# A BitNet attention and feed-forward layer on eight cores: deferred transposes, a third weight buffer, and PSUM copies moved to ScalarE

## The reference

```python
xn = _layernorm(x)
x = x + attention(xn, Wq, Wk, Wv, Wo) + ffn(xn, gate_w, up_w, down_w, gate_s, up_s, down_s)

def bitlinear(x, W):      # ternary weights, 8-bit activations per row
    sw = mean(abs(W)) + 1e-05
    Wq = clip(round(W / sw), -1, 1) * sw
    sx = 127 / clip(max(abs(x), axis=-1, keepdims=True), 1e-05, None)
    xq = clip(round(x * sx), -128, 127) / sx
    return einsum('bsd,od->bso', xq, Wq)
# attention: q = rope(bitlinear(x, Wq)), k = rope(bitlinear(x, Wk)), v = bitlinear(x, Wv);
#            16 query heads, 4 key/value heads of 128; causal softmax; bitlinear(out, Wo)
# ffn:       g = (x @ gate_w.T) * gate_s;  u = (x @ up_w.T) * up_s      (inner width 5632)
#            out = ((silu(g) * u) @ down_w.T) * down_s
```

## Time and profile before

| | us |
|---|---|
| median of 2 runs | 5812.83 |
| the 2 runs | 5696.64, 5929.02 |
| profiled execution, whole | 5710.21 |
| its slowest core (core 1), span | 5708.6 |
| its other cores, spans | 5672.5 to 5704.6 |

### The profile page before, as it was taken

The page is one execution under the profiler, slowest core; times in us unless marked ns, Lnnn a source line. Parts: engine busy times, 40 slices in busy tenths (PEclk is TensorE's granted clock), DMA queues, the critical chain, the costliest instruction groups (busy, mean ns, idle before and its releaser), DMA issues.

```text
span 5708.6 us, 54936 instructions; the slowest of 8 cores (5672.5 to 5708.6 us)
## 1 busy us (share of the span) xinstructions
PE 3868.1 (68%) x18728; PEld 1777.5 (31%) x18728; DVE 1691.8 (30%) x2717; ACT 1640.2 (29%) x1375; POOL 303.1 (5%) x276
## 2 busy tenths in 40 slices
PE   1899988889999886044443034445788889973068
PEld 1344434434444343032332023333222222222034
DVE  4100000000000001455555456555422211137433
ACT  4111110001111000443332421220455656653231
POOL 0111110011111000000000000000000000000000
PEclk9899999999999998567676567778999999985589
DMA  3578867768786775411112611111000000000656
GB/s 120 56 70 79 76 65 83 83 69 78 74 78 66 85 83 87 130 50 52 50 65 62 175 57 34 44 45 49 15 10 8 7 6 5 6 3 1 184 191 215
DMA packets 800203, 387.61 MB, mean 68 GB/s; under 512 B 552256, under 2 KB 777920, under 8 KB 787648
## 3 DMA queue, kind: packets, MB, share of 16 engines
q0 software_dynamic: 548608, 161.50, 26.7%
q1 hardware_dynamic: 251328, 222.61, 13.1%
HBM read 480.53 MB, written 41.94 MB: 92 GB/s over the span
## 4 chain that ended last, share of the span: by engine, by line
PE 55%; DVE 19%; DMA 10%; ACT 9%; issue 5%; DVEq 1%; ACTq 0%; SPq 0%; POOLq 0%; POOL 0%
PE f_pd_h L341 11%; PE f_pg_h L300 11%; PE f_pu_h L306 11%; PE c_pse L736 3%; PE c_ppv L740 3%; ACT c_pp L794 2%; PE e_po L943 2%; PE c_psc L785 2%; DMA wq_wb<-wq_t 2%; PE c_psc L783 2%; DMA wo_wb<-wo_t 2%; PE c_pse L738 2%; PE c_ppv L742 2%; PE b_pkv L554 2%; DVE b_mx L165 2%
## 5 line engine op out<-in xcount | busy, mean ns | idle before, releaser
L794 ACT ACTIVATE c_pp<-c_psc 128x1024 bf16<-128x1024 f32 x640 | 656.0, 1025 | 582.9 <-PE c_psc L785 582.9
L341 PE MATMUL f_pd_h<-hdnT,f_dw_h 128*128 128x512 bf16 x2816 | 639.1, 390 | 45.9 <-DMA f_dw_h<-dw_t 45.9
L300 PE MATMUL f_pg_h<-xnT,f_gw_h 128*128 128x512 bf16 x2816 | 639.4, 386 | 31.1 <-DMA f_uw_h<-uw_t 31.1
L306 PE MATMUL f_pu_h<-xnT,f_uw_h 128*128 128x512 bf16 x2816 | 635.3, 385 | 0.0
L803 DVE TENSOR_TENSOR c_pp<-c_pp,cmask 128x512 bf16<-128x512 bf16 x512 | 217.7, 425 | 799.9 <-ACT c_pp L794 770.9
L651 PE MATMUL b_pq<-b_xqT,qtern 128*128 128x256 bf16 x2048 | 270.5, 292 | 266.9 <-DVE b_qrot L660 258.3
L321 DVE TENSOR_TENSOR hdnT<-f_sg_h,f_su_h 128x1024 bf16<-128x1024 bf16 x88 | 61.0, 693 | 1219.0 <-ACT f_su_h L317 1219.0
L341 PEld LDWEIGHTS f_pd_h<-hdnT,f_dw_h 128*128 128x128 bf16 x2816 | 283.5, 101 | 391.9 <-issue 81.0
L300 PEld LDWEIGHTS f_pg_h<-xnT,f_gw_h 128*128 128x128 bf16 x2816 | 279.4, 99 | 376.6 <-issue 79.4
L306 PEld LDWEIGHTS f_pu_h<-xnT,f_uw_h 128*128 128x128 bf16 x2816 | 278.5, 99 | 342.4 <-issue 43.4
L532 PE MATMUL b_pkv<-b_xqT,ktern 128*128 128x256 bf16 x1024 | 177.4, 355 | 289.4 <-DVE b_krot L541 272.6
(11 more groups left out here) (163 smaller groups left out, 4013.2 us busy)
## 6 DMA issues: line engine op xcount, KB each, us to landing
f_gw_h<-gw_t POOLq DMA_DIRECT2D x88, 512.0 KB, 6.8
f_uw_h<-uw_t POOLq DMA_DIRECT2D x88, 512.0 KB, 8.8
f_dw_h<-dw_t POOLq DMA_DIRECT2D x32, 1408.0 KB, 16.6
b_xch<-x_kv SPq DMA_DIRECT2D x16, 2048.0 KB, 7.8
wq_wb<-wq_t SPq DMA_DIRECT2D x32, 1024.0 KB, 6.8
wo_wb<-wo_t SPq DMA_DIRECT2D x32, 1024.0 KB, 6.8
f_xch<-x_q SPq DMA_DIRECT2D x4, 4096.0 KB, 16.5
ffn_scr<-f_ffs_h SPq DMA_DIRECT2D x32, 512.0 KB, 10.6
```

The source lines that it names most:

```text
L300: e.matmul(pg[:, bi, tc * 512:(tc + 1) * 512], gwb[bi][:, dt, :], xnT[:, dt, half * HT + tc * 512: half * HT + (tc + 1) * 512], start=(dt ...
L306: e.matmul(pu[:, bi, tc * 512:(tc + 1) * 512], uwb[bi][:, dt, :], xnT[:, dt, half * HT + tc * 512: half * HT + (tc + 1) * 512], start=(dt ...
L341: e.matmul(pd[:, bi, tc * 512:(tc + 1) * 512], dwb[bi][:, it, :], hdnT[:, it, tc * 512:(tc + 1) * 512], start=(it == 0), stop=(it == NIT - 1))
L794: E("scalar", lambda e, k0=k0, sbk=sbk: e.activation(pp[:, (k0 % 8):(k0 % 8) + 2, :].rearrange("p a b -> p (a b)"), psc[sbk][:], AF.Exp, s ...
```

## The change

- F2 has three buffers each for the gate and up weights, F3 three for the down weights (`i % 3`, `h % 3`), with three semaphores each. The PSUM halves and the store buffers keep two.
- In F3 the transposes, the copies to `ffstage` and the store of step `h` become a function `f3tail` that is issued after block `h+1` (and before ACT's copy of step `h+1`); the last step's tail is issued at the end of the half. The transpose groups wait for the last copy out of their own bank (`ptf_ve[g]`), not for the newest DVE count.
- `emit_tr16` can copy out with ACT (`evac_eng="scalar"`). B1 and B2 use it so; F1 and D stay on DVE. In B1 the copy of V to `vT` is on ACT too. The lists that say when a PSUM bank is free now hold (semaphore, count) pairs.

The core of the diff:

```diff
-    def emit_tr16(src, dst_fn, ptr, src_ready_w, tag_rot, ptr_ve=None, extra_w=()):
+    def emit_tr16(src, dst_fn, ptr, src_ready_w, tag_rot, ptr_ve=None, extra_w=(),
+                  evac_eng="vector"):
...
-            E("vector", lambda e, g=g, bank=bank: e.tensor_copy(
-                dst_fn(g), bank.rearrange("p (a b) -> p a b", b=128)),
-              waits=[(pe, pe.n)], inc=(ve, 1))
...
+            else:
+                E("scalar", lambda e, g=g, bank=bank: e.activation(
+                    dst_fn(g), bank.rearrange("p (a b) -> p a b", b=128), AF.Identity),
+                  waits=[(pe, pe.n), (ac, ac.n)], inc=(ac, 1))
+                if ptr_ve is not None:
+                    ptr_ve[bi] = (ac, ac.n)
...
-                    gwb = [sb(f"f_gw{i}_h{half}", [128, NDT, 128], BF16, f2) for i in range(2)]
-                    uwb = [sb(f"f_uw{i}_h{half}", [128, NDT, 128], BF16, f2) for i in range(2)]
+                    gwb = [sb(f"f_gw{i}_h{half}", [128, NDT, 128], BF16, f2) for i in range(3)]
+                    uwb = [sb(f"f_uw{i}_h{half}", [128, NDT, 128], BF16, f2) for i in range(3)]
...
-                          waits=[(pe, wpe[bi])] + (fence if i < 2 else []), inc=(s_gw[bi], 16))
+                          waits=[(pe, wpe[wb])] + (fence if i < 3 else []), inc=(s_gw[wb], 16))
...
-                          waits=[(pe, dpe[bi])] + (fence3 if h < 2 else []), inc=(s_dw[bi], 16))
+                          waits=[(pe, dpe[wb])] + (fence3 if h < 3 else []), inc=(s_dw[wb], 16))
...
+                        dpe[wb] = pe.n
+                        if f3pend[0] is not None:
+                            f3pend[0]()
+                            f3pend[0] = None
+                        E("scalar", lambda e, h=h, pb=pb: e.activation(fft[:], pd[:, pb, :], AF.Identity,
                                                                        scale=c_ds[:, h:h + 1]),
                           waits=[(pe, pe.n)], inc=(ac, 1))
...
+                        def f3tail(h=h, pb=pb, half=half, FOK=FOK):
+                            for g in range(2):
+                                E("tensor", lambda e, g=g: [
+                                    e.transpose(ptf[:, g % 2, j * 128:(j + 1) * 128],
+                                                fft[:, (g * 4 + j) * 128:(g * 4 + j + 1) * 128],
+                                                c_identf[:]) for j in range(4)][-1],
+                                  waits=[FOK, (ve, ptf_ve[g]), (s_fst[pb], stv[pb])], inc=(pe, 1))
+                                E("vector", lambda e, g=g, pb=pb: e.tensor_copy(
+                                    ffstage[pb][:, g * 4:(g + 1) * 4, :].rearrange("p a b -> p (a b)"),
+                                    ptf[:, g % 2, :]),
+                                  waits=[(pe, pe.n)], inc=(ve, 1))
+                                ptf_ve[g] = ve.n
+                            E("sync", lambda e, h=h, pb=pb, half=half: e.dma_start(
...
+                        f3pend[0] = f3tail
...
-                                  ptr, rdy, t, ptr_ve)
+                                  ptr, rdy, t, ptr_ve, evac_eng="scalar")
...
-                    XQT = (ve, ve.n)
+                    XQT = (ac, ac.n)
...
-                        E("vector", lambda e, t=t, c=c, pb=pb: e.tensor_copy(
-                            vT[:, c * 2 + t, :], pkv[pb][:]),
-                          waits=[(pe, pe.n), (ve, ve.n)], inc=(ve, 1))
-                        pkv_ve[pb] = ve.n
+                        E("scalar", lambda e, t=t, c=c, pb=pb: e.activation(
+                            vT[:, c * 2 + t, :], pkv[pb][:], AF.Identity),
+                          waits=[(pe, pe.n), (ac, ac.n)], inc=(ac, 1))
+                        pkv_ve[pb] = (ac, ac.n)
```

More of the change, by code:

```diff
@@ L195, in emit_tr16 @@
             bank = ptr[:, bi, :]
-            war = (ve, ptr_ve[bi]) if ptr_ve is not None else (ve, ve.n)
+            war = ptr_ve[bi] if ptr_ve is not None else (ve, ve.n)
             E("tensor", lambda e, g=g, bank=bank, src=src: [
@@ L289, in do_half @@
                         bi = i % 2
-                        E("gpsimd", lambda e, i=i, bi=bi: e.dma_start(
-                            out=gwb[bi][:], in_=gw_t[:, i * 128:(i + 1) * 128]
+                        wb = i % 3
+                        E("gpsimd", lambda e, i=i, wb=wb: e.dma_start(
+                            out=gwb[wb][:], in_=gw_t[:, i * 128:(i + 1) * 128]
                             .rearrange("(t p) f -> p t f", p=128)),
-                          waits=[(pe, wpe[bi])] + (fence if i < 2 else []), inc=(s_gw[bi], 16))
-                        E("gpsimd", lambda e, i=i, bi=bi: e.dma_start(
-                            out=uwb[bi][:], in_=uw_t[:, i * 128:(i + 1) * 128]
+                          waits=[(pe, wpe[wb])] + (fence if i < 3 else []), inc=(s_gw[wb], 16))
+                        E("gpsimd", lambda e, i=i, wb=wb: e.dma_start(
+                            out=uwb[wb][:], in_=uw_t[:, i * 128:(i + 1) * 128]
                             .rearrange("(t p) f -> p t f", p=128)),
[L297 to L300, removed]
+                          waits=[(pe, wpe[wb])] + (fence if i < 3 else []), inc=(s_uw[wb], 16))
+                        wready = [(s_gw[wb], s_gw[wb].n), (s_uw[wb], s_uw[wb].n)]
+                        E("tensor", lambda e, bi=bi, wb=wb, half=half: [
+                            e.matmul(pg[:, bi, tc * 512:(tc + 1) * 512], gwb[wb][:, dt, :],
                                      xnT[:, dt, half * HT + tc * 512: half * HT + (tc + 1) * 512],
@@ L304, in do_half @@
                           waits=wready + [(ac, silu_ac[bi])] + (fence if i < 2 else []), inc=(pe, 1))
-                        E("tensor", lambda e, bi=bi, half=half: [
-                            e.matmul(pu[:, bi, tc * 512:(tc + 1) * 512], uwb[bi][:, dt, :],
+                        E("tensor", lambda e, bi=bi, wb=wb, half=half: [
+                            e.matmul(pu[:, bi, tc * 512:(tc + 1) * 512], uwb[wb][:, dt, :],
                                      xnT[:, dt, half * HT + tc * 512: half * HT + (tc + 1) * 512],
@@ L324, in do_half @@
                 with f3:
-                    dwb = [sb(f"f_dw{i}_h{half}", [128, NIT, 128], BF16, f3) for i in range(2)]
+                    dwb = [sb(f"f_dw{i}_h{half}", [128, NIT, 128], BF16, f3) for i in range(3)]
                     fft = sb(f"f_fft_h{half}", [128, HT], F32, f3)
@@ L348, in do_half @@
+                        E("scalar", lambda e, h=h, pb=pb: e.activation(fft[:], pd[:, pb, :], AF.Identity,
                                                                        scale=c_ds[:, h:h + 1]),
                           waits=[(pe, pe.n)], inc=(ac, 1))
-                        fft_ac[bi] = ac.n
+                        fft_ac[pb] = ac.n
                         FOK = (ac, ac.n)
[L352 to L367, removed]
+                        def f3tail(h=h, pb=pb, half=half, FOK=FOK):
[8 more added lines that the diff above has]
+                                    ptf[:, g % 2, :]),
+                                  waits=[(pe, pe.n)], inc=(ve, 1))
+                                ptf_ve[g] = ve.n
+                            E("sync", lambda e, h=h, pb=pb, half=half: e.dma_start(
+                                out=ffn_scr[half * HT:(half + 1) * HT, h * 128:(h + 1) * 128]
+                                .rearrange("(a p) b -> p a b", p=128),
+                                in_=ffstage[pb][:]),
+                              waits=[(ve, ve.n)], inc=(s_fst[pb], 16))
+                            stv[pb] = s_fst[pb].n
@@ L534, in mms_b1 @@
                             for dt in range(NDT)][-1],
-                          waits=[XQT, (ve, pkv_ve[pb])], inc=(pe, 1))
+                          waits=[XQT, pkv_ve[pb]], inc=(pe, 1))
                         E("vector", lambda e, pb=pb, cb=cb: e.tensor_tensor(
@@ L653, in mms_b2 @@
                             for dt in range(NDT)][-1],
-                          waits=[XQT, (ve, pq_ve[pb])], inc=(pe, 1))
+                          waits=[XQT, pq_ve[pb]], inc=(pe, 1))
                         E("vector", lambda e, pb=pb, cb=cb: e.tensor_tensor(
```

59 lines of the change are left out of this document (32 added, 27 removed).

## The result

| | before | after |
|---|---|---|
| median | 5906.18 us (10 runs, 5696.64 to 6059.18) | 5782.9 us (11 runs, 5528.98 to 5867.98) |
| ratio, undisturbed executions | | 0.9691, 95% interval 0.9589 to 0.9793 |
| profiled execution | 5710.21 us | 5528.98 us |
| core 4, span | 5677.7 us | 5527.4 us |

A die is four of the cores, 0 to 3 or 4 to 7. In most executions of either kernel one die, or both, was granted less clock (a mean of 0.79 to 0.85 in place of 0.86), which adds some 100 to 400 us; the ratio leaves those out, the medians do not.

What follows compares the result with a forecast made beforehand. PE bounds gate/up, holes of 3.7 us lengthen the down stage's periods, and DVE and ACT wait on each other in B1. Terms +4 +4 -122 -34 -1 = -149 took 5710 to 5561 us, range 5510 to 5650.

Steps and rivals of the forecast that it cites:

- Sum: Whole kernel: +4 +4 -122 -34 -1 = -149 from the profiled 5710, giving 5561 us for executions like that one.
- rival A: Feed-forward: the clock takes the gain back; down period 24.2 us, 5689 in all, some 5925 if all runs slow; chance 0.09.
- B1: Copies moved to ACT: path from V matmuls to next mean 11.1 us instead of 13.39, -34 us in all.
- Down stage: Deferred tail closes the hole between blocks: period 19.93 us instead of 23.99, -122 us over both halves.
- Third buffer: Feed-forward weight loads: no steady wait to remove; first loads sharing costs +4 us in gate/up and +4 in down.
- rival D: Starts of the four feed-forward stages: loads collide at their worst (+5, +5, +8, +8), 5579 us; no chance given.
- B2: Copies moved to ACT: next load issued 8.5 us after the last rotation instead of 8.60, -1 us over 8 chunks.
- Rivals B and C: B: down loads and stores share DMA, 5623 us; C: ACT's order wins nothing in B1, 5595 to 5600; either 0.17.

Runs made afterwards that it cites:

- e_tail: The kernel before with the down stage's deferred tail alone, two weight buffers, copies on DVE; ratio 0.9767 (0.956 to 0.9974), lowest 5572.14 us.
- z_zero: The kernel after with its feed-forward input set to zero, plus one fill on DVE; six executions, 5574 to 5588 us.
- z_after: The kernel after, unchanged, run again beside the kernel before and its own zero-data copy; six executions, 5582 to 5917 us.

## Why the prediction missed, point by point

- **The median: wrong.** The step that failed is the end of "Sum", "the forecast is for executions like it", with 0.09 for rival A: the lower clock was put at nothing in the sum. The runs showed it in ten of the twelve executions of that series whose clocks are on record, and the median came out 222 us above the forecast. The two runs shown before took 5697 and 5929 us, and a range for the time had to hold both kinds. Rival A's price for the down stage was right (24.2 us a period; the cores of `e_tail` at 0.81 show 24.16) but it was tied to the wrong condition: it was to come if the *denser* down stage held the level. The runs show it coming to either kernel, by the moment and the chip, in gate/up, down, B1, B2, attention and E, and in the feed-forward only with real data. What picks the moment stays open. The Trainium skill (TensorE: Matmul & The Clock Gate, Seeing it yourself) says of its current limit that all-zero operands do not trip it; `z_zero` agrees, 0 of 12 dies against 6 of 12. It also says that the whole die goes to that level; in `z_after` cores 6 and 7 had 0.86 in that stretch while 4 and 5 of their die had 1.00. No execution with a whole die low for long was profiled.
- **The profiled execution: 181 us gained for 149, partly by luck.** Of the 32, 14 lay in the profile before, which was that much above the lowest time of its kernel; the other 18 are sizes of terms: B1 12 more than taken, the buffers 5, down 2, within a microsecond.
- **Down stage: right.** Period 19.87 against 19.93, blocks back to back, (23.99 - 19.87) x 30 = 124 against 122. What the sum did not see is its make-up: of the 4.12, 1.2 were the needless wait for a copy (1051.87 - 1050.18 - 0.46), 1.1 as a mean the lower level at the start of two blocks in three (periods of 24.3 to 24.6 us beside 22.88), and 1.8 the ACT copy and its handovers (21.63 - 19.87).
- **Third buffer: right that it wins nothing.** +4 was taken for down and +3 measured as a mean of the cores, with 14 on core 4, close to rival D's worst for down (16); for gate/up +4 was taken and nothing found (29.7 to 28.3).
- **B1: right mechanism, 34 taken, 46 measured.** Mis-sized: the transposes of tile 1 were ready 0.76 us after their start, not 1.1, since their granted clock is 1.00 here and was 0.50 before (in this chunk those of tile 0 follow the V matmuls without a pause); the V copy takes 0.60, not 0.67. 10.3 us for the path, not 11.1, which is the 12 us over 15 chunks.
- **B2: right.** -1 taken, 0 measured on core 4; 8.5 us from the last rotation to the load's issue, as forecast; 1.03 us for a copy taken, 1.023 measured.
- **Rivals B and C** did not come. With two buffers there are waits for loads of up to 2.7 us in some periods; whether the store or only the issue time causes them was not tried.

## What to carry to other kernels

A wait for an engine's newest count, where only one bank matters, can cost a period twice: here 1.2 us by the wait and 1.1 by the clock after the longer pause. Work moved to an idle engine wins only where the chain ends in it, and its queue then orders what else ends there: look at what stands behind it. A forecast of a measured time must say which clock it assumes, and a spread of 4% between two runs before is a fact to be predicted, not noise to be put aside.

## What the runs showed of the hardware

The clock in the feed-forward hangs on the data: with zero input six executions of the kernel after lay within 14 us, with real data on the same chip within 334. The level of 0.81 came to cores in pairs (0 and 1, 2 and 3, 4 and 5, 6 and 7): in `e_tail` it held cores 4 and 5 from 553 us on for 159 us, while 6 and 7 had it only after 3700 us. After a pause of 3.7 us between blocks two of three started at 0.50, after one of 2.5 us none. With a load of 1408 KB issued whole in step 40, PE waited 5 to 15 us, core by core, for the 512 KB of the next steps; with it in eleven pieces over as many steps it did not wait there.
